# Fp32 passes with four column blocks to a bank, and an attention group's stages further apart in them

## The reference, cut to what matters

```python
target = item_table[item_id] + gelu(LN(item_emb @ mm_w + mm_b))
seq_emb = item_table[item_seq]                       # 50 gathered rows per sample
x = concat([t, seq_emb, t - seq_emb, t * seq_emb])
scores = relu(x @ aw1 + ab1) @ aw2 + ab2             # masked where item_seq == 0
hist_feat = einsum('bs,bsd->bd', softmax(scores), seq_emb)
sparse = stack([like, view, item_id, item_img, hist])        # 5 fields of 128
se = sparse * sigmoid(relu(mean(sparse) @ se_w1 + se_b1) @ se_w2 + se_b2)
bil = [(se_i @ bil_W[i]) * se_j for i < j]                   # 10 fields of 128
dnn_in = concat([se, bil])                                   # 15 x 128 = 1920 columns
xc = dnn_in
for i in range(2):
    xc = dnn_in * (xc @ cross_K[i] + cross_bias[i]) + xc     # 1920 x 1920, twice
h = gelu(LN(xc @ w1 + b1)); h = gelu(LN(h @ w2 + b2)); out = sigmoid(h @ w3 + b3)
```

## Time and profile before

| | us |
|---|---|
| runs shown: median (lowest to highest) | 2124.95 (2123.55 to 2125.77) |
| the profiled execution | 2128.74 |
| its span | 2126.7 |
| PE busy | 1971.2 (93%) |
| PEld busy | 1590.0 (75%) |
| DVE busy | 1284.6 (60%) |
| POOL busy | 886.0 (42%) |
| ACT busy | 864.8 (41%) |

### The profile page before, as it was taken

The page is one execution under the profiler, slowest core; times in us unless marked ns, Lnnn a source line. Parts: engine busy times, 40 slices in busy tenths (PEclk is TensorE's granted clock), DMA queues, the critical chain, the costliest instruction groups (busy, mean ns, idle before and its releaser), DMA issues. The chain is left out here.

```text
span 2126.7 us, 34665 instructions
## 1 busy us (share of the span) xinstructions
PE 1971.2 (93%) x10733; PEld 1590.0 (75%) x10733; DVE 1284.6 (60%) x2216; ACT 864.8 (41%) x1868; POOL 886.0 (42%) x854
## 2 busy tenths in 40 slices
PE   4478888987899999999999999999999999999997
PEld 3256877776677787777777887777777888888886
DVE  4544444346677755667778766667778654445553
ACT  1532222224444434564445344654544334322234
POOL 7777646564775700547575400647560000000000
PEclk7588999999999999999999999999999999999998
DMA  8333434333343552334344452334332354233320
GB/s 244 116 83 106 123 103 118 109 103 103 99 133 103 145 186 82 91 96 134 112 128 121 119 193 74 95 96 142 116 107 87 106 179 130 88 96 97 99 67 1
DMA packets 108484, 240.95 MB, mean 113 GB/s; under 512 B 22784, under 2 KB 27920, under 8 KB 108176
## 3 DMA queue, kind: packets, MB, share of 16 engines
q1 hardware_dynamic: 72144, 157.54, 24.3%
q0 software_dynamic: 27136, 55.63, 10.2%
q10 hardware_dynamic: 9024, 25.57, 3.3%
HBM read 225.87 MB, written 12.79 MB: 112 GB/s over the span
## 5 line engine op out<-in xcount | busy, mean ns | idle before, releaser
L487 POOL DMA_INDIRECT e<-in_item_table,idx_all x800 | 838.4, 1048 | 680.5 <-POOLq L507 450.4
L1297 DVE TENSOR_TENSOR Wl<-raw,Wh 128x640 fp32r<-128x640 f32 (+1 forms) x366 | 295.0, 806 | 258.3 <-DVEq L1296 256.9
L945 ACT ACTIVATE Wh<-raw 128x640 fp32r<-128x640 f32 (+1 forms) x366 | 261.2, 721 | 447.9 <-ACTq L944 441.5
L657 PE MATMUL psum<-X1h,Wh 128*128 128x512 f32 x900 | 357.3, 397 | 0.6 <-PEq L655 0.6
L658 PE MATMUL psum<-X1l,Wh 128*128 128x512 f32 x900 | 350.9, 390 | 0.0
L659 PE MATMUL psum<-X1h,Wl 128*128 128x512 f32 x900 | 350.4, 389 | 0.0
L657 PE MATMUL psum<-X0h,Wh 128*128 128x512 f32 x675 | 270.4, 401 | 0.0
L658 PE MATMUL psum<-X0l,Wh 128*128 128x512 f32 x675 | 263.3, 390 | 0.0
L659 PE MATMUL psum<-X0h,Wl 128*128 128x512 f32 x675 | 263.2, 390 | 0.0
L914 ACT ACTIVATE e<-e,pw 128x128 f32<-128x128 f32 x800 | 242.8, 388 | 15.1 <-ACTq L171 15.1
L1247 DVE TENSOR_REDUCE hist<-e 128x128 f32<-128x1280 f32 (+1 forms) x65 | 155.9, 2398 | 74.7 <-DVEq L1245 74.7
(11 more groups left out here) (163 smaller groups left out, 2590.7 us busy)
## 6 DMA issues: line engine op xcount, KB each, us to landing
raw<-in_cross_K SPq DMA_DIRECT2D x399, 320.0 KB
raw<-in_w SPq DMA_DIRECT2D x51, 256.0 KB
e<-in_item_table,idx_all POOLq DMA_INDIRECT x800, 2.5
dnn_scratch<-dn ACTq DMA_DIRECT2D x12, 960.0 KB, 4.3
kept<-in_cross_K SPq DMA_DIRECT2D x24, 320.0 KB, 3.8
x1f<-dnn_scratch ACTq DMA_DIRECT2D x3, 2048.0 KB, 9.1
x1f<-dnn_scratch ACTq DMA_DIRECT2D x3, 1792.0 KB, 14.9
e<-in_w SPq DMA_DIRECT2D x9, 256.0 KB, 4.6
```

What stands on the lines that cost most here:

```text
L487: nc.gpsimd.indirect_dma_start(out=dst, out_offset=None, in_=table, in_offset=bass.IndirectOffsetOnAxis(ap=idx_all[:, t, s:s + 1], axis=0) ...
L657: m0 = mm(out, wh, Xh[:, 0:T, k, :], start=(k == 0), stop=False)
L945: af(Wh[:, split_slot(w), 0:n], raw[:, rs, 0:n], ACT.Copy).then_inc(hi_done, 1)
L1297: v.tensor_tensor(Wl[:, rs, 0:n], raw[:, rs, 0:n], Wh[:, slot, 0:n].bitcast(F32), ALU.subtract).then_inc(lo_done, 1)
```

## The change

It has three parts. The fp32 columns go four to a bank: block n of a pass stands at columns 128 (n mod 4) of bank `bank(a, n // 4)`, TensorE waits for a bank and tells of its end once for four blocks (three in a pass's last quad), and VectorE scales the four one after the other at the next step. The solo steps get step functions of their own on three engines, with a new order. And a group's stages lie further apart there: transposes at k, `hidden` at k + 2, `score` at k + 3, softmax, exponentials and weighing at k + 4, `history` at k + 5. Outside the solo steps they stay at k, k + 1, k + 2. `SPREAD` now places tile 5 as well, and `GROUP_STEPS[0]` only tiles 6 and 7, from steps 60 and 66 on (before: tile 5 at 53 to 57, tile 6 at 59 to 63, tile 7 at 65 to 69).

```diff
-FULL = 2 * (TPC - 1)
-HALVES = {FULL + 2 + q: (2 * q, 2 * q + 1) for q in range(FEATS // 2)}
-SPREAD = ((-2, 0, 1, 3, 5), (8, 11, 14, 17, 20), (23, 26, 29, 32, 35), (38, 41, 44, 47, 50))
+QUAD = 4
+QUADS = -(-FEATS // QUAD)
+HALVES = {9: (0, 1, 2), 10: (3, 4), 11: (5, 6), 12: (7,), 13: (8, 9), 14: (10, 11)}
+SPREAD = ((-2, 0, 2, 4, 6), (8, 11, 14, 17, 20), (23, 26, 29, 32, 35), (38, 41, 44, 46, 48), (50, 52, 54, 56, 58))
-    0: [[s + g for g in range(NG)] for s in (8, 14, 20)],
+    0: [[s + g for g in range(NG)] for s in (15, 21)],
 (make_plan, for a group at a solo step k)
+            elif k + 2 < solo_end:
+                plan[k + 2].open = plan[k + 3].score = plan[k + 4].summed = (t, g)
+                done = k + 4
+                if done < solo_end:
+                    done += 1
+                    plan[done].hist = (t, g)
 (a tile's head and tail)
+        elif s <= solo_end:
+            fetch, aim, swing, share, neg = s - 6, s - 4, s - 1, s, s + 1
-        gate = last + 2 if t < OPEN else last + 3
-        plan[last + 2].fold = plan[gate].gate = plan[gate + 1].lift = plan[gate + 2].pair = t
+        gate = done if t < TILES[0] + 1 or t == TILES[0] + TILES[1] - 1 else done + 1
+        plan[done].fold = plan[gate].gate = plan[gate + 1].lift = plan[gate + 2].pair = t
 (TensorE)
-                out = xps[:, bank(a, n), 0:P]
-                if kg == 0:
+                q, r = divmod(n, QUAD)
+                out = xps[:, bank(a, q), r * P:(r + 1) * P]
+                if kg == 0 and r == 0:
                     pe.wait_ge(bank_free, 1).then_inc(bank_free, -1)
-                if kg == UNITS - 1:
+                if kg == UNITS - 1 and (r == QUAD - 1 or n == FEATS - 1):
                     last.then_inc(mm_done, 1)
+            def solo_step(p):
+                solo_products(p.solo, p.n, 0)
+                if p.open: hidden()
+                if p.pair is not None: tail_bilinear(p.pair)
+                if p.grp: transposes10(*p.grp)
+                solo_products(p.solo, p.n, 1)
+                if p.swing is not None: head_turn()
+                solo_products(p.solo, p.n, 2)
+                if p.share is not None: head_share(p.share)
+                if p.score: score()
+                if p.lift is not None: tail_turn(p.lift)
 (ScalarE's solo_step, the order of the calls)
+                tail_copy, head_fetch, copy_eT10, copy_tT, exps, weigh, tail_gate, x_hi of p.split, three w_hi where not early, tail_store
 (VectorE)
+            def solo_quad(a, q):
+                ns = range(QUAD * q, min(QUAD * q + QUAD, FEATS))
+                dve.wait_ge(mm_done, 1).then_inc(mm_done, -1)
+                for n in ns:
+                    r = n % QUAD
+                    last = v.scalar_tensor_tensor(out=x1f[:, a, n, :], in0=xps[:, bank(a, q), r * P:(r + 1) * P], scalar=col("cb", n),
+                                                  in1=x0f[:, a, n, :], op0=ALU.add, op1=ALU.mult)
+                done(last)
+                dve.sem_inc(bank_free, 1)
+                if a == PASSES and q:
+                    dve.sem_inc(xnew_ready, 2 * QUAD if q == 1 else len(ns))
 (VectorE's solo_step, the order of the calls)
+                solo_quad, head_neg, softmax_max, hidden_max, tail_pairs, history, tail_fold, tail_gate_apply, x_lo of p.split, times_target, head_aim, three w_lo where not early
```

More of the change, by code:

```diff
@@ L135, in make_plan @@
         plan += [Step(c, k) for k in range(STEPS)]
-    where = []
+    where, paired = [], []
     for j in range(OPEN):
@@ L1042, in opening_step, with solo_step @@
                     images_gelu()
+            def solo_step(p):
+                c, k = p.chunk, p.k
+                if p.pair is not None:
+                    tail_copy(p.pair)
+                if p.fetch is not None:
+                    head_fetch(p.fetch)
+                if p.grp:
+                    copy_eT10()
+                if p.swing is not None:
+                    copy_tT(p.swing)
+                if p.summed:
+                    exps(*p.summed)
+                    weigh(*p.summed)
+                if p.gate is not None:
+                    tail_gate()
+                for n in p.split:
+                    x_hi(c, 0, n)
+                if not p.early:
+                    for q in range(UNITS):
+                        unit(c, UNITS * k + q)
+                if p.pair is not None and p.pair >= TILES[0]:
+                    tail_store(p.pair)
             def step(p):
+                if p.solo is not None:
+                    solo_step(p)
+                    return
                 c, k, T = p.chunk, p.k, p.fc
@@ L1054, in step @@
                     tail_copy(p.pair)
-                if not p.early:
-                    unit(c, 3 * k)
+                unit(c, 3 * k)
                 if p.fetch is not None:
@@ L1065, in step @@
                     copy_eT10()
-                if p.gate is not None:
+                if p.gate is not None and p.gate != p.fold:
                     tail_gate()
-                if not p.early:
-                    unit(c, 3 * k + 1)
+                unit(c, 3 * k + 1)
                 if T and 2 <= k < T + 2:
@@ L1084, in step @@
                     fc_sd(T)
+                if p.gate is not None and p.gate == p.fold:
+                    tail_gate()
             def w1_stage(c):
@@ L1448, in step @@
                     h1_rest(c - 1)
[L1449 to L1453, removed]
+                unit(c, 3 * k)
+                for quad in p.quads:
+                    solo_quad(*quad)
+                if p.prev:
                     x_scale(*p.prev)
-                if not p.early:
-                    unit_out(c, 3 * k)
+                unit_out(c, 3 * k)
                 if T and 3 <= k < T + 3:
```

131 lines of the change are left out of this document (92 added, 39 removed).

## The result

The changed kernel takes 2073.39 us (median of four runs, 2071.52 to 2074.13), the kernel before 2125.36 beside it: a ratio of 0.9755, interval 0.9738 to 0.9772. It is faster, by 52 us, where I had forecast 81. The profiled execution is 2074.13 us with a span of 2071.2; the forecast, made on that scale, was a span of 2045.5, so 25.7 us are to be explained.

What follows compares the result with a forecast made beforehand. The 60 fp32 steps lose 67.9 us to TensorE idle and 37 to low clock. 124.2 + 283.1 + 8 + 73 = 488.3 against 573.9 gains 85.6, less 4.4 is 81.2: 2043 us, range 2018 to 2071.

Steps and rivals of the forecast that it cites:

- The step that failed: Two-step groups (tile 1, from step 44): VectorE's 7.3 us of work per group fits the 11.3 us of room.
- steps 54 to 60: Last fp32 steps and step 60: 73 us with waits on ScalarE's and VectorE's line, 51 without a wait.
- Up to step 53: fp32 steps before 54: 283.1 us of work plus 8 us of waits and low clock.
- Four blocks to a bank: fp32 products up to step 53: TensorE's 30.0 us of idle ahead of them go to zero, at no cost.
- 104.3 us: Today's idle plus low clock in the fp32 stretch: 427.7 us less 323.4 us of work.
- After step 60: Later steps that TensorE fills: one group moved there gives back 4.4 us; fold and gate at step 72 stay covered.
- Rival 2: fp32 steps: half of today's 104 us stays, through late gathers or VectorE's line in two-step rows; 2071 us, chance 0.17.
- Rival 1: fp32 steps and step 60: waits vanish altogether, steps 54 to 60 at 51 us; 30 us better, 2013, chance 0.10.
- Rival 3: fp32 stretch: the mean clock stays 0.92 even without long waits; +20 us, 2063, chance 0.10.
- Rival 4: Dense fp32 stretch is granted 1.2 GHz for good: slower, 2350 us with all work at low clock; chance 0.02.
- Rival 5: fp32 products: a bank wait is left for every block, gain only from the distances, about 40 us; 2085, chance 0.03.
- the signs set down beforehand: Before step 53: product idle under 8 us, `hidden` not waiting, clock 0.97; then one or two idles over 4 us.

Runs made afterwards that it cites:

- the mended order: Changed kernel with X1h ahead of exponentials and weighing, X1l behind times_target, bilinear at the step's end, hidden behind the second third of products: 2054.13 us, 0.9661.
- all orders at once: Changed kernel with every order move together, tile 4's gate one step after its fold, and step 60's first split weight ahead of history: 2061.2 us, 0.9703.
- the weights split early: Kernel of 2054.1 us with step 60's three split weights made at the end of step 58 instead of step 59: 2057.53 us, 0.9679.
- the shared bank taken away again: Kernel of 2054.1 us with hidden's last 128 columns written over its first 128, not into the scores' bank: 2051.75 us, 0.9647.
- the evenly spread one: Kernel of 2054.1 us with the groups of tiles 3 to 5 placed more evenly over the passes: 2055.75 us, 0.9667.

## Why the prediction was wrong: right in direction, too low by 30 us

**The step that failed** is "With a group every two steps (tile 1, and from step 44) the room is 11.3 us for the same 7.3 us, and it still closes". The 7.3 us are VectorE's sum, and the only meeting point I held against it was `teT`. I left out the second thing that `hidden` waits for, `hscore_free`, which stands in the code that moved (L595). Moving `score` from the step of `hidden` to the step before the next `hidden` took the room at this semaphore, where groups are two steps apart, from more than a step to some 3 us: 2.0 us of waits in the first steps, 11.4 in steps 54 to 60, and low clock behind the two long ones. Without it the kernel is 14 us faster, which is over half of the 25.7 us. Of the 11.2 us by which the term "steps 54 to 60" was too small, 8.5 go with it (75.7 us against the 73 forecast). The term's other waits came about as large as priced (first `Wl` 7.5 against some 10, bilinear 3.5 against 5), and step 60 itself took 17.6 for 19.5. The first `Wl` was simply later for both sides: TensorE went on with it 66.6 us after the start of step 54 where I had 53.5, and 57.7 without the shared bank. The distance of two steps is not all of it: in the mended order, spreading the groups evenly took this wait from 6.1 to 2.1 us, though more of them then stand two steps apart. In the two long waits it is a fold and gate, or a head and an `X1l`, that stand ahead of softmax; I had listed them in the same forecast and not held them against this semaphore.

**Up to step 53** I had 8 us and it was 18.5 (301.6 less the 283.1 of work): 10.9 us in waits and some 8 of low clock (0.03 x 301.6 = 9 by the rows). The work was right to a few tenths, 14.76 us for three steps with one group against 14.7. The idle is the bilinear of tile 1 at step 13, 4.7 us, behind the weighing on ScalarE; I described just this for step 55 and did not look for it in the two-step stretch of tile 1. `tail_turn` was 4.2 us in three waits where I said about 1. The timeline of ScalarE in step 13, with the copy that the bilinear waits for:

```profile
202.10 3.03 ACT L962 ACTIVATE e<-e,pw 128x128 f32<-128x128 f32 x10 [0.19 <-ACTq L199]
205.03 0.68 ACT L979 ACTIVATE x0f<-psum 128x640 f32<-128x640 f32 x1
```

That this is the mechanism is shown by moving the bilinear: 4.8 of its 6 us are won up to step 53. Moving `X1h` says nothing of step 13, since there is no `X1h` yet; 5.7 of its 7 us are won in steps 54 to 60.

**Four blocks to a bank: right in the row, wrong in its worth.** "The 30.0 us go to zero" held. But the prediction counted them as gained, and the banks alone give 8, on top of the rest about 4, which the noise does not tell from none. The idle time at a semaphore is not what the semaphore costs, where the next one on the path waits for the same late line.

**A third owner of idle time** was left out: 30.0 and 28.1 of the 67.9 us are two, and 9.8 stood in four waits ahead of `head_share` (L586, the wait for the bank that it shares with the bilinear). The banks alone leave it (11.6 in five waits); in the changed kernel, where the steps of a tile's head have moved too, it is gone. The sum counted it within its 104.3 us, so the forecast did not suffer by it. Two slips of the pen change nothing either: 3.43 + 1.09 + 1.04 + 3.43 + 1.15 is 10.1, and 2043 + 310 is 2353.

**After step 60** 8.3 us are given back instead of 4.4: the group moved there costs 5.1 by step 73, 2.0 are the three small idles in and after step 74, said to be hidden, and about 1 is unassigned; executions of one kernel differ by as much.

**The rivals.** Rival 2, the waits that move instead of going, was the right one, in its time (2071) and nearly in its terms: it had 52 us of idle time and low clock in the 60 steps and 20 us for step 60, measured are 49.2 (368.2 less 319.0) and 17.6. I gave it 0.17. Of its two causes VectorE's line in the two-step rows held, late gathers did not (L572 has 0.0 idle); the semaphore where the waits turned up it did not name. Rival 1 fell. Rival 3 fell where TensorE is kept busy: 0.97 up to step 53 and 1.00 in the full round. Rival 4 fell with it. Rival 5 fell: the bank is not waited for. Of the signs set down beforehand, the idle time ahead of the products and the clock came as written; `hidden` still waited 2.0 us before step 53; and the idles over 4 us in steps 54 to 60 were three, of which only the last stood where I had put it.

**Open.** The kernel of 2054.1 us has 70 us in steps 54 to 60 (422.6 to 492.6) where the work is 51.3. Each wait of it that was taken away was nearly made up by the next, so I take VectorE's and ScalarE's line, with twelve columns to split beside two-step groups, for the bound. That is argued from three kernels (all orders at once, the weights split early, the shared bank taken away again) and not shown: the one kernel that thins this line out, the evenly spread one, has these steps 12 us shorter in its profile, and those before them 7 us longer, and is no faster in its median. Nor was a kernel tried in which ScalarE's copy of `eT` goes behind the exponentials at the far distances.

## What to carry to other kernels

When a stage is moved, list every semaphore that its instructions wait for, not only its input: a buffer that it shares, here one PSUM bank for two small results, can turn from a formality into the wait that decides. Price a wait by what the same late engine will hold up next, and try its removal alone: 30 us of idle time at one place were worth 8 and then 4. And when a schedule closes only by the distance between stages, its places can't be taken without it: the same places with near stages were 3% slower than the kernel before with ScalarE's new order, and 1.6% with the old one.

## What the runs showed of the hardware

Behind the long idle pieces TensorE works at its low clock for a while. The ten transposes take 2.40 us at 434.35, after 4.17 us idle, against 1.25 at 305.87; the three matmuls of a split product 0.63 us each behind the 7.46 us idle of step 60, against 0.39 four microseconds later. By the mean clocks the low clock before step 60 cost about 34 us before and 18 after, so some 16 of the 59.9 us gained there came back through it. The Trainium skill (TensorE: Matmul & The Clock Gate, Part 1) puts the ramp under 1% of a typical span; by the mean clock of the rows it is 0.03 x 301.6 + 0.14 x 84.2 = 21 us here, 1.0%, and it was 1.7% before: not a term to leave out.

The last 128 columns of `hidden` and the scores never overlap, and still the program lets the write wait for the read. The Trainium skill (PSUM — Partial Sum Buffer, PSUM bank collisions raise a hardware error) asks for PSUM to be guarded by bank and quadrant and not by address, and by that rule the wait is needed; no run here shows a collision. What the wait costs two runs show: 14 us in the changed kernel, and 2 to 3, within the noise, once the order was mended.
